# Attention with its shifted scores between the weighings, key blocks added in pairs on GpSimd, and a feed-forward stage written out without a loop

## The chip, the cores and the metric

The kernel runs on one core of a Trainium2 chip. The metric is the device time of one execution in microseconds (us). Of the kernel before, three runs gave 2557.92, 2559.57 and 2560.83 us, a median of 2559.57 us.

## The reference

One transformer layer with adaptive layer norms. `x` has 4 batches of 1024 rows of 512 numbers, there are 16 heads of 32, and the hidden width is 2048. Everything is fp32. Cut to what matters:

```python
h = layernorm(x) * (1 + ca) + sa
q = rotary((layernorm(h) @ Wq + bq) * scale, h); k, v = ...   # same for keys
qn, kn = layernorm(q), layernorm(k)                            # over each head's 32
scores = einsum('bhqd,bhkd->bhqk', qn, kn) / sqrt(32)
scores = where(causal, scores, -max)
a = softmax(scores) @ v
x = x + ga * (a @ Wo + bo)
h = layernorm(x) * (1 + cb) + sb
x = x + gb * ((silu(h @ w_gate.T) * (h @ w_up.T)) @ w_down.T)
```

## The kernel before

Each stage is a block of its own with one hand-written instruction stream per engine, tied by semaphores: setup and query/key/value projection, attention (`attention_stage`, about 443 to 1299 us of the span), output projection with the second layer norm, and the feed-forward stage (`ffn_stage`, from 1466 us to the end).

**Attention** works on 16 groups (one batch, four heads), one round per group. A round has 12 steps. In step `w` TensorE does, for the current group, two score items (`score`, L739, into the PSUM slots of `b_psA`); VectorE takes the maximum of each over its keys (`peak`, L820). For the group before, 14 steps later (`SHIFT_LAG`), it computes the scores again transposed and shifted by each row's maximum, one (half of the queries, block of 128 keys) per step, four heads (`shift`, L760 and L763, into the two buffers of `b_psB`); ScalarE takes the exponential of each head into `b_probT` (`exponent`, L887). One step later TensorE multiplies these weights with the values (`weigh(.., False)`, output `b_psO`) and with ones (`weigh(.., True)`, output `b_psL`, the sum of the weights, which is the softmax's divisor), both on L778. A block is 512, 384, 256 or 128 queries wide, by the causal mask: over the 12 blocks of a round six are 512 wide and two each have the other widths. The four heads lie in four column strips of the array, 32 columns each.

The order on TensorE in a step is: shift of heads 0 and 1, score, shift of heads 2 and 3, score, in steps 1 and 3 also eight transposes for the next group (`prepare`, L724), then the two products of `weigh`. After the last block of a half VectorE copies `b_psO` out (`take`, L836), in steps 7 and 3; it does so behind the first `peak` of its step. The transposes use a slot of `b_psA`, are widened on ScalarE (`widen`, L876), split into high and low part on GpSimd (`high`, L691) and VectorE (`low`, L813). The slots of `b_psA` are two and go round over scores, transposes and maxima, so each waits for the reader of the one before the last. When the sums of a group are out, GpSimd issues a chain of DMAs that turns them for a reciprocal and spreads the result (`normalise`, L695 to L705), and multiplies the output.

**Feed-forward** takes 8 row blocks of 512 rows; each goes over 16 hidden chunks of 128. A chunk is 24 matmuls for gate and up (`matrix`, L1286 to L1288) and, two chunks later, 12 for the down product (`down`, L1274 to L1276), which add up in `f_psD` over the 16 chunks. ScalarE does silu (L1217) and the high part of the product (L1212), VectorE the product (L1227) and its low part (L1231), GpSimd the split of the down weights. The loop over blocks is a hardware loop with peeled ends (`stagger`). At the border of two blocks the next block's rows are split all at once (`split_h`, L1207 and L1238) into the only buffer `f_hT_hi`/`f_hT_lo`, once the last chunk's up product is done; the last `down` of a block comes one chunk earlier than the others (`down_last`), and the end of a block (`final`, L1248 and L1250) scales and adds four tiles in turn, with two buffers for the scaled ones.

Of the kernel before, what the change touches and what calls it, by code (L numbers as in the profile page):

```python
# [26 lines left out]
P = 128  # L27
# [488 lines left out]
def attention_stage(nc, args, scratch):  # L516
# [12 lines left out]
    BUFS = 3  # L529

# [21 lines left out]

    def take_at(k):
# [15 lines left out]
    with ExitStack() as ctx:  # L569
# [3 lines left out]
        def sem(name):  # L573
# [18 lines left out]
        probT = sb("b_probT", [P, 3, 4, W])  # L592
# [9 lines left out]
                 "peaks_turned peaks_copied peaks_in shifted expd weighed summed taken_o taken_l sums_out few_in inverted few_out "  # L602
# [17 lines left out]
        def _(sp):  # L620
# [36 lines left out]

            load(0)
# [4 lines left out]
            for k in STEPS:  # L663
                n, w = unit(k)
                if peaks_at(k) is not None:
                    lay_peaks(peaks_at(k))
                if w == 4 and n + 2 < NG:
                    load(n + 2)
                if w == 4 and n + 1 < NG:
                    lay_stacks(n + 1)  # L670
                if w == 5 and 0 <= n < NG:
                    load_v(n)
                if w == 10 and 0 <= n - 2 < NG:
                    store(n - 2)
# [3 lines left out]
        def _(pool):  # L678
# [13 lines left out]

            def normalise(n):
                pool.wait_ge(s["taken_l"], 2 * n + 2)
                pool.dma_start(scratch["sums"][0], sums[0:P:HD, n % 2]).then_inc(s["sums_out"], 16)  # L695
                pool.wait_ge(s["sums_out"], 16 * n + 16)
                pool.dma_start(few[:, 0], scratch["sums"][0].rearrange("j (a c) -> (j a) c", c=C // HD)).then_inc(s["few_in"], 16)
                pool.wait_ge(s["inverted"], n + 1)
                pool.dma_start(scratch["sums"][1].rearrange("j (a c) -> (j a) c", c=C // HD), few[:, 1]).then_inc(s["few_out"], 16)
                pool.wait_ge(s["few_out"], 16 * n + 16)  # L700
                for j in range(4):
                    pool.dma_start(sums[j * HD:(j + 1) * HD, n % 2], scratch["sums"][1, j:j + 1].broadcast_to([HD, C])).then_inc(s["wide_in"], 16)
# [4 lines left out]
            for k in STEPS:  # L707
                if prep_at(k):
                    high(*prep_at(k))
                at = take_at(k)  # L710
                if at and at[1] == 1 and at[0] < NG - 1:
                    normalise(at[0])

        @block.tensor
        def _(pe):
# [50 lines left out]
            def weigh(n, w, summing):  # L766
                half, kb = BLOCKS[w]
                if not summing:
                    pe.wait_ge(s["expd"], 4 * (NW * n + w) + 4)
                    if w == 0:  # L770
                        pe.wait_ge(s["v_in"], 16 * n + 16)
                if kb == 0:
                    at_least(pe, s["taken_l" if summing else "taken_o"], 2 * n + half)
                first = max(kb, half * HALF)
                out = psL if summing else psO
                for j in range(4):
                    rows = slice(j * HD, (j + 1) * HD)
                    mm = pe.matmul(out[rows, (first - half * HALF) * P:W], ones[:] if summing else v[:, n % 2, kb, rows],  # L778
                                   probT[:, (NW * n + w) % 3, j, 0:(half + 1) * W - first * P],
                                   start=(kb == 0), stop=(kb == (half + 1) * HALF - 1), skip_group_check=True)  # L780
                mm.then_inc(s["summed" if summing else "weighed"], 1)

            for k in STEPS:
# [7 lines left out]
                if prep_at(k):  # L791
                    prepare(*prep_at(k))
                if peaks_at(k) is not None:
                    turn_peaks(peaks_at(k))
                if weigh_at(k):
                    weigh(*weigh_at(k), False)
                    weigh(*weigh_at(k), True)

        @block.vector
        def _(dve):  # L800
# [48 lines left out]
            for k in STEPS:  # L849
# [10 lines left out]
                at = take_at(k - 5)  # L860
                if at and at[1] == 1 and at[0] < NG - 1:
                    dve.wait_ge(s["few_in"], 16 * at[0] + 16)
                    dve.reciprocal(few[:, 1], few[:, 0]).then_inc(s["inverted"], 1)
                at = take_at(k)
# [4 lines left out]
        def _(act):  # L869
# [9 lines left out]
            def exponent(n, w, j):  # L879
# [3 lines left out]
                if j == 0:  # L883
                    at_least(act, s["summed"], NW * n + w - 2)
                    at_least(act, s["weighed"], NW * n + w - 2)
                width = (half + 1) * W - max(kb, half * HALF) * P
                act.activation(probT[:, (NW * n + w) % 3, j, 0:width], psB[:, i % 2, 0:width], ACT.Exp).then_inc(s["expd"], 1)  # L887
# [6 lines left out]
            def take(n, half):  # L894
                act.wait_ge(s["summed"], NW * n + (HALF if half == 0 else NW))
# [3 lines left out]
            for k in STEPS:  # L899
                for j in range(4):  # L900
                    if shift_at(k):
                        exponent(*shift_at(k), j)
                    if j == 1 and take_at(k):
                        take(*take_at(k))
# [207 lines left out]
def ffn_stage(nc, args, scratch, w_hi, w_lo, out):  # L1112

    NB = NT // 4
    T = 4 * P
    HC = HID // P
    with ExitStack() as ctx:
# [3 lines left out]
        def sem(name):  # L1123
# [3 lines left out]
        hT_hi = sb("f_hT_hi", [P, KC, T], F32R)  # L1127
        hT_lo = sb("f_hT_lo", [P, KC, T], F32R)
# [8 lines left out]
        scaled = sb("f_scaled", [P, 2, DM])  # L1137
        x1 = sb("f_x1", [P, 4, DM])
        spots = sb("f_spots", [1, 4])
        still = sb("f_still", [1, 1])  # L1140
# [4 lines left out]
        names = ("gate_in h_in h_hi h_lo gate_mm up_mm silu gu gu_hi gu_lo wd_hi wd_lo down "  # L1145
                 "scaled final still").split()
        s = {n: sem("f_" + n) for n in names}
        wd_in = [sem(f"f_wd_in{j}") for j in range(2)]
        x1_in = sem("f_x1_in")
# [3 lines left out]
        def done(i, c):  # L1153
            return i * HC + (c + 1)

        @block.sync
        def _(sp):
            def load_h(i, c):
                if c == 0:
                    at_least(sp, s["h_lo"], KC * i)  # L1160
# [201 lines left out]
```

## Time and profile before

| | |
|---|---|
| median of 3 runs | 2559.57 us |
| profiled execution | 2558.22 us |
| its span | 2556.4 us |
| mean granted TensorE clock | 0.964 |
| TensorE matmul busy | 2351.2 us (92%) |
| VectorE busy | 1178.3 us (46%) |
| ScalarE busy | 787.0 us (31%) |
| GpSimd busy | 752.0 us (29%) |

Busy time is the time in which an engine had at least one instruction under way. Matmuls overlap each other by their modelled ends, so on TensorE the distance from one start to the next says what an instruction costs, and its own duration does not. "Granted clock" is the share of TensorE's full clock in that stretch.

### The profile page before, as it was taken

The page shows a single profiled execution, that of the slowest core. Times are in us where ns is not written, and L with a number is a line of the kernel's source. Part 1 is how long each engine was busy: PE and PEld are TensorE (multiplying, and loading weights), DVE is VectorE, ACT ScalarE, POOL GpSimd, SP SyncE. Part 2 cuts the span into 40 slices and gives each one's busy share as a digit, 9 for nine tenths or more (in the row PEclk, how much of TensorE's full clock was granted, in tenths as well). Part 3 has the DMA queues.
Part 4 walks back from the last instruction along what each step waited for, and adds up shares of the span by engine and source line. Part 5 has one row for each costly group of instructions (what it writes and reads, how often), then busy time and mean ns, then how long its engine had stood idle before and what let it go on. Part 6 is the DMA issues. An engine that isn't in the chain of part 4 may idle for free. (4 is left out here: it accounts for less than half of the span.)

```text
span 2556.4 us, 33412 instructions
## 1 busy us (share of the span) xinstructions
PE 2351.2 (92%) x12504; PEld 1699.5 (66%) x12504; DVE 1178.3 (46%) x1806; ACT 787.0 (31%) x1659; POOL 752.0 (29%) x822
## 2 busy tenths in 40 slices
PE   2899995599999999999958799999999999999998
PEld 0677774466566566556436578787878787878787
DVE  4799996545555555555349721212121212121212
ACT  1333331054454545544535511111111111111111
POOL 1477776001211111121156322222222222222221
PEclk7899997589999999999989999999999999999999
DMA  5122222636545544643058721212121121212111
GB/s 181 59 99 99 98 90 104 140 76 146 122 102 126 134 110 108 140 118 89 19 172 295 259 83 31 87 33 78 38 66 49 45 70 45 70 46 69 41 59 36
DMA packets 162516, 244.80 MB, mean 96 GB/s; under 512 B 17205, under 2 KB 84373, under 8 KB 161902
## 3 DMA queue, kind: packets, MB, share of 16 engines
q1 hardware_dynamic: 153898, 222.23, 30.0%
q0 software_dynamic: 7456, 18.07, 2.6%
q10 hardware_dynamic: 1064, 3.18, 0.3%
q8 instruction: 64, 1.05, 0.2%
q14 instruction: 34, 0.28, 0.0%
HBM read 133.28 MB, written 59.28 MB: 75 GB/s over the span
## 5 line engine op out<-in xcount | busy, mean ns | idle before, releaser
L820 DVE TENSOR_REDUCE b_top<-b_psA 128x2 f32<-128x1024 f32 (+3 forms) x384 | 363.4, 957 | 289.6 <-PE b_psA L739 165.7
L887 ACT ACTIVATE b_probT<-b_psB 128x512 f32<-128x512 f32 (+3 forms) x768 | 339.7, 491 | 349.4 <-PE b_psB L763 234.0
L1227 DVE TENSOR_TENSOR f_gu<-f_psU,f_silu 128x512 f32<-128x512 f32 x128 | 88.5, 691 | 749.3 <-PE f_psU L1288 749.3
L760 PE MATMUL b_psB<-b_stack 98*128 98x512 f32 (+3 forms) x768 | 288.0, 414 | 6.3 <-ACT b_probT L887 4.9
L739 PE MATMUL b_psA<-b_stack 96*128 96x512 f32 (+3 forms) x768 | 256.6, 392 | 28.6 <-DMA b_stack<-b_halves 20.3
L760 PEld LDWEIGHTS b_psB<-b_stack 98*128 98x128 f32 x768 | 140.1, 189 | 190.1 <-issue 118.5
L57 POOL TENSOR_TENSOR f_spots<-f_still 1x1 f32<-1x1 f32 x128 | 25.9, 202 | 795.1 <-PE f_psD L1276 788.8
L1217 ACT ACTIVATE f_silu<-f_psG 128x512 f32<-128x512 f32 x128 | 76.6, 598 | 523.5 <-PE f_psG L1288 523.5
L1274 PE MATMUL f_psD<-f_wd_hi,f_gu_hi 128*128 128x512 f32 x512 | 201.1, 393 | 22.8 <-DVE f_gu_lo L1231 12.3
L1286 PE MATMUL f_psG<-f_hT_hi,w_hi 128*128 128x512 f32 x512 | 200.4, 391 | 11.1 <-DVE f_hT_lo L1238 11.1
L1276 PE MATMUL f_psD<-f_wd_hi,f_gu_lo 128*128 128x512 f32 x512 | 200.0, 391 | 0.0
L1287 PE MATMUL f_psG<-f_hT_hi,w_lo 128*128 128x512 f32 x512 | 199.9, 390 | 0.0
L1275 PE MATMUL f_psD<-f_wd_lo,f_gu_hi 128*128 128x512 f32 x512 | 199.8, 390 | 0.0
L1288 PE MATMUL f_psG<-f_hT_lo,w_hi 128*128 128x512 f32 x512 | 199.7, 390 | 0.0
L1287 PE MATMUL f_psU<-f_hT_hi,w_lo 128*128 128x512 f32 x512 | 199.2, 389 | 0.0
L1288 PE MATMUL f_psU<-f_hT_lo,w_hi 128*128 128x512 f32 x512 | 199.2, 389 | 0.0
L1286 PE MATMUL f_psU<-f_hT_hi,w_hi 128*128 128x512 f32 x512 | 199.2, 389 | 0.0
L1212 ACT ACTIVATE f_gu_hi<-f_gu 128x512 fp32r<-128x512 f32 x128 | 80.8, 631 | 358.3 <-DVE f_gu L1227 358.3
L739 PEld LDWEIGHTS b_psA<-b_stack 96*128 96x128 f32 x768 | 145.8, 201 | 45.7 <-issue 21.7
L1196 POOL TENSOR_TENSOR f_wd_lo<-f_wd,f_wd_hi 128x512 fp32r<-128x512 f32 x128 | 167.9, 1311 | 10.7
L778 PE MATMUL b_psO<-b_probT,b_v 128*32 128x512 f32 (+3 forms) x1536 | 164.3, 500 | 3.7 <-DVE b_att L836 2.8
L507 PE MATMUL a_psQ<-wqkv_hi,hT_hi 128*128 128x512 f32 x384 | 162.1, 422 | 0.0
(165 smaller groups left out, 4229.0 us busy)
## 6 DMA issues: line engine op xcount, KB each, us to landing
b_stack<-b_halves SPq DMA_DIRECT2D x192, 256.0 KB, 5.0
f_wd<-in_wd_t SPq DMA_DIRECT2D x128, 256.0 KB, 2.6
qkv_d<-a_t SPq DMA_DIRECT2D x32, 512.0 KB, 2.6
b_land<-qkv_d SPq DMA_DIRECT2D x32, 512.0 KB, 4.7
a_x<-in_x SPq DMA_DIRECT2D x32, 256.0 KB, 3.2
qkv_d<-a_v SPq DMA_DIRECT2D x32, 256.0 KB, 2.9
b_v<-qkv_d SPq DMA_DIRECT2D x16, 512.0 KB, 5.8
att_d<-b_att SPq DMA_DIRECT2D x16, 512.0 KB, 3.2
```

What stands on the lines that cost most here:

```text
L739: mm = pe.matmul(out[:, h, 0:hi - lo], stack[0:ROWS, n % BUFS, 1, j, t * P:(t + 1) * P], stack[0:ROWS, n % BUFS, 0, j, lo:hi], start=True, ...
L760: mm = pe.matmul(psB[:, i % 2, cols], stack[0:NR, n % BUFS, 0, j, kb * P:(kb + 1) * P], stack[0:NR, n % BUFS, 1, j, first * P:(half + 1) * ...
L778: mm = pe.matmul(out[rows, (first - half * HALF) * P:W], ones[:] if summing else v[:, n % 2, kb, rows], probT[:, (NW * n + w) % 3, j, 0:(h ...
L820: dve.tensor_reduce(out, slot("score", NI * n + i)[:, :, 0:width], AX.X, ALU.max, negate=True).then_inc(s["maxed"], 1)
L887: act.activation(probT[:, (NW * n + w) % 3, j, 0:width], psB[:, i % 2, 0:width], ACT.Exp).then_inc(s["expd"], 1)
L1196: pool.tensor_tensor(wd_lo[:, c % 2], wd[:, c % 2], wd_hi[:, c % 2].bitcast(F32), ALU.subtract).then_inc(s["wd_lo"], 1)
L1274: pe.matmul(out_t, gu_hi[:, c % 2, cols], wd_hi[:, c % 2], start=first, stop=False)
L1275: pe.matmul(out_t, gu_hi[:, c % 2, cols], wd_lo[:, c % 2], start=False, stop=False)
L1276: last = pe.matmul(out_t, gu_lo[:, c % 2, cols], wd_hi[:, c % 2], start=False, stop=end)
L1286: pe.matmul(out_c, w_hi[:, m, k, cols], hT_hi[:, k], start=(k == 0), stop=False)
L1287: pe.matmul(out_c, w_lo[:, m, k, cols], hT_hi[:, k], start=False, stop=False)
L1288: last = pe.matmul(out_c, w_hi[:, m, k, cols], hT_lo[:, k], start=False, stop=(k == KC - 1))
```

## The change

There are three edits in the attention stage and one rewrite of the feed-forward stage.

First, in a step `weigh` now stands behind the first score, between the two pairs of shifted scores; transposes and maxima stay behind the second score. Second, GpSimd adds the weights of the second key block of each pair into those of the first (`add_pair`, six adds a round, over 384, 128, 512, 512, 384 and 128 columns of each of four heads), and TensorE multiplies the sum with ones once for both (`add_up`), at the end of the even steps, three steps after the pair's second block. `b_probT` gets five buffers for three. Third, the DMAs of `normalise` move from GpSimd's queue to SyncE's (steps 6, 7, 9 and 10), its multiplication to step 11, the reciprocal to step 8, the store to step 2; the copy of the sums (`take` on ScalarE) comes two steps later.

In the feed-forward stage the loop is written out over all 128 chunks. `f_hT_hi` and `f_hT_lo` get two buffers, and the next block's split is spread over chunks 8 to 11. All `down` products come two chunks behind. The four scalings stand in chunk 1 of the next block, each behind its own tile's last matmul, the four additions in chunk 2, with four buffers. The rows to add land in `f_land`, which the split has left free by then.

```diff
+    PROBS = 5
+    def sum_at(k):
+        return pair_at(k - 3)
+    def take_sum_at(k):
+        return take_at(k - 2)
...
+            def add_pair(n, i):
...
+                pool.wait_ge(s["weighed"], NW * n + 2 * i + 1)
+                pool.wait_ge(s["expd"], 4 * (NW * n + 2 * i + 1) + 4)
+                pool.tensor_tensor(into, into, probT[:, (at + 1) % PROBS, :, 0:width], ALU.add).then_inc(s["added"], 1)
...
+            def add_up(n, i):
+                half, kb = BLOCKS[2 * i]
+                pe.wait_ge(s["added"], NW // 2 * n + i + 1)
+                if kb == 0:
+                    at_least(pe, s["taken_l"], 2 * n + half)
+                first = max(kb, half * HALF)
+                for j in range(4):
+                    mm = pe.matmul(psL[j * HD:(j + 1) * HD, (first - half * HALF) * P:W], ones[:],
...
-                if prep_at(k):
-                    prepare(*prep_at(k))
-                if peaks_at(k) is not None:
-                    turn_peaks(peaks_at(k))
-                if weigh_at(k):
-                    weigh(*weigh_at(k), False)
-                    weigh(*weigh_at(k), True)
+                    if i == 1 and prep_at(k):
+                        prepare(*prep_at(k))
+                    if i == 1 and peaks_at(k) is not None:
+                        turn_peaks(peaks_at(k))
+                    if i == 0 and weigh_at(k):
+                        weigh(*weigh_at(k))
+                if sum_at(k):
+                    add_up(*sum_at(k))
...
-        hT_hi = sb("f_hT_hi", [P, KC, T], F32R)
-        hT_lo = sb("f_hT_lo", [P, KC, T], F32R)
+        hT_hi = sb("f_hT_hi", [P, 2, KC, T], F32R)
+        hT_lo = sb("f_hT_lo", [P, 2, KC, T], F32R)
...
-            stagger(dve, NB, HC, [(product, 1), (split_h, 0), (low, 1), (final, 2)])
+            for u in range(NU + 3):
+                i, c = u // HC, u % HC
+                if 1 <= u <= NU:
+                    product(u - 1)
+                    low(u - 1)
+                if i < NB - 1 and 8 <= c < 8 + KC:
+                    split_h(i + 1, c - 8)
+                if c == 1 and 1 <= i <= NB:
+                    for t in range(4):
+                        scale(i - 1, t)
+                        if i == NB:
+                            add(i - 1, t)
+                if c == 2 and 1 <= i < NB:
+                    for t in range(4):
+                        add(i - 1, t)
...
-            stagger(pe, NB, HC, [(down_early, 2), (down_last, 1), (gate_up, 0)])
+            for u in range(NU + 2):
+                if u >= 2:
+                    down(u - 2)
+                if u < NU:
+                    at_least(pe, s["silu"], u - 1)
+                    matrix(u, 0)
+                    at_least(pe, s["gu"], u - 1)
+                    matrix(u, 1)
```

TensorE's queue in step 7 of a round, before (the names are the tiles of the text; L760 shift, L739 and L742 score, L778 the two products, first block of the second half):

```order
L760 MATMUL b_psB<-b_stack 128x512 [waits b_expd] x2
L739 MATMUL b_psA<-b_stack 128x384 [waits b_maxed]
L742 MATMUL b_psA<-b_mask_r,b_ident_r 128x128
L739 MATMUL b_psA<-b_stack 128x384
L742 MATMUL b_psA<-b_mask_r,b_ident_r 128x128
L760 MATMUL b_psB<-b_stack 128x512 [waits b_expd] x2
L739 MATMUL b_psA<-b_stack 128x512 [waits b_maxed]
L742 MATMUL b_psA<-b_mask_r,b_ident_r 128x128
L739 MATMUL b_psA<-b_stack 128x512
L742 MATMUL b_psA<-b_mask_r,b_ident_r 128x128
L778 MATMUL b_psO<-b_probT,b_v 32x512 [waits b_taken_o,b_expd]
L778 MATMUL b_psO<-b_probT,b_v 32x512 x3
```

The same step in the changed kernel (L800 shift, L779 and L782 score, L816 the product with the values):

```order
L800 MATMUL b_psB<-b_stack 128x512 [waits b_expd] x2
L779 MATMUL b_psA<-b_stack 128x384 [waits b_maxed]
L782 MATMUL b_psA<-b_mask_r,b_ident_r 128x128
L779 MATMUL b_psA<-b_stack 128x384
L782 MATMUL b_psA<-b_mask_r,b_ident_r 128x128
L816 MATMUL b_psO<-b_probT,b_v 32x512 [waits b_taken_o,b_expd]
L816 MATMUL b_psO<-b_probT,b_v 32x512 x3
L800 MATMUL b_psB<-b_stack 128x512 [waits b_expd] x2
L779 MATMUL b_psA<-b_stack 128x512 [waits b_maxed]
L782 MATMUL b_psA<-b_mask_r,b_ident_r 128x128
L779 MATMUL b_psA<-b_stack 128x512
L782 MATMUL b_psA<-b_mask_r,b_ident_r 128x128
```

The product with the values, and with it the wait for `b_taken_o` (VectorE's copy of `b_psO`), has moved from the end of the step to directly behind its first score. VectorE's queue at that place is the same in both kernels, here of the changed one (L871 the maxima, L887 the copy); the last of the seven maxima is that of the step's first score:

```order
L871 TENSOR_REDUCE b_top<-b_psA 128x2 [waits b_scored] x7
L887 COPY b_att<-b_psO 128x512 [waits b_stored,b_scaled,b_weighed]
L871 TENSOR_REDUCE b_top<-b_psA 128x2 [waits b_scored] x3
L914 RECIPROCAL b_few<-b_few 128x32 [waits b_few_in]
```

VectorE's queue at the border of two feed-forward blocks, before (L1248 scaling, L1250 addition, L1227 product, L1231 its low part):

```order
L1248 TENSOR_TENSOR f_scaled<-f_psD,f_gate 128x512 [waits f_down,f_x1_in,f_gate_in]
L1250 TENSOR_TENSOR f_x<-f_x,f_scaled 128x512 [waits f_scaled]
L1248 TENSOR_TENSOR f_scaled<-f_psD,f_gate 128x512
L1250 TENSOR_TENSOR f_x<-f_x,f_scaled 128x512 [waits f_scaled]
L1248 TENSOR_TENSOR f_scaled<-f_psD,f_gate 128x512 [waits f_final]
L1250 TENSOR_TENSOR f_x<-f_x,f_scaled 128x512 [waits f_scaled]
L1248 TENSOR_TENSOR f_scaled<-f_psD,f_gate 128x512 [waits f_final]
L1250 TENSOR_TENSOR f_x<-f_x,f_scaled 128x512 [waits f_scaled]
```

And in the changed kernel (L1310 scaling, L1315 addition, L1296 product, L1300 its low part):

```order
L1310 TENSOR_TENSOR f_scaled<-f_psD,f_gate 128x512 [waits f_down_t,f_gate_in]
L1310 TENSOR_TENSOR f_scaled<-f_psD,f_gate 128x512 [waits f_down_t] x2
L1310 TENSOR_TENSOR f_scaled<-f_psD,f_gate 128x512 [waits f_down]
L1296 TENSOR_TENSOR f_gu<-f_psU,f_silu 128x512 [waits f_gu_hi,f_silu,f_up_mm]
L1300 TENSOR_TENSOR f_gu_lo<-f_gu,f_gu_hi 128x512 [waits f_gu_hi]
L1315 TENSOR_TENSOR f_land<-f_land,f_scaled 128x512 [waits f_scaled,f_x1_in] x4
```

The four scalings no longer alternate with the additions, and the additions come a chunk later.

## Rows read from the trace of the kernel before

**Rows 1.** Each engine by stretch: start:end, length, busy, PE clock, DMA.

```profile
700.00:800.00 100.00, 98.87 (x750) 59.91 (x752) 54.82 (x66) 49.69 (x107) 17.10 (x21) 1.00 0.49 118
1600.00:1700.00 100.00, 96.73 (x426) 79.48 (x425) 24.62 (x36) 16.59 (x28) 25.14 (x36) 1.00 0.21 64
```

**Rows 2.** TensorE in time, a block border: start, us, engine, line, operation, count.

```profile
1602.91 0.39 PE L1276 MATMUL f_psD<-f_wd_hi,f_gu_lo 128*128 128x512 f32 x1
1605.07 0.50 PE L1274 MATMUL f_psD<-f_wd_hi,f_gu_hi 128*128 128x512 f32 x1 [1.77 <-DVE f_gu_lo L1231]
...
1618.58 0.39 PE L1288 MATMUL f_psU<-f_hT_lo,w_hi 128*128 128x512 f32 x1
1620.46 0.47 PE L1274 MATMUL f_psD<-f_wd_hi,f_gu_hi 128*128 128x512 f32 x1 [1.50 <-DVE f_scaled L1248]
```

**Rows 3.** ScalarE in time, two chunks of the feed-forward stage.

```profile
1626.22 0.60 ACT L1217 ACTIVATE f_silu<-f_psG 128x512 f32<-128x512 f32 x1 [3.91 <-PE f_psG L1288]
1634.38 0.60 ACT L1217 ACTIVATE f_silu<-f_psG 128x512 f32<-128x512 f32 x1 [4.08 <-PE f_psG L1288]
```

**Rows 4.** The chain that ended last: start, us, engine, tile, line.

```profile
2548.22 0.24 PE f_psD L1276
...
2553.29 0.69 DVE f_x L1250
```

**Rows 5.** GpSimd in time, once a round, two rounds.

```profile
764.46 1.04 POOL L691 TENSOR_SCALAR b_halves<-b_whole 128x1024 fp32r<-128x1024 f32 x1 [12.22 <-ACT b_whole L876]
...
813.87 1.04 POOL L691 TENSOR_SCALAR b_halves<-b_whole 128x1024 fp32r<-128x1024 f32 x1 [12.40 <-ACT b_whole L876]
```

**Rows 6.** TensorE in time, step 9 of a round.

```profile
793.14 0.99 PE L760 MATMUL b_psB<-b_stack 98*128 98x512 f32 x2
...
794.32 0.23 PE L742 MATMUL b_psA<-b_mask_r,b_ident_r 128*128 128x128 f32 x1
794.48 1.06 PE L778 MATMUL b_psO<-b_probT,b_v 128*32 128x512 f32 x8
795.36 1.04 PE L778 MATMUL b_psL<-b_probT,b_ones 128*32 128x512 f32 x8
796.33 0.50 PE L760 MATMUL b_psB<-b_stack 98*128 98x512 f32 x1
```

**Rows 7.** TensorE and VectorE in time, step 3 of a round.

```profile
767.95 0.73 PE L739 MATMUL b_psA<-b_stack 96*128 96x512 f32 x2
768.72 1.23 DVE L820 TENSOR_REDUCE b_top<-b_psA 128x2 f32<-128x1024 f32 x1 [0.49 <-PE b_psA L739]
769.86 0.68 DVE L836 COPY b_att<-b_psO 128x512 f32<-128x512 f32 x1
770.00 1.09 PE L724 MATMUL b_psA<-b_ident,b_land 128*128 128x128 f32 x8 [0.32 <-DVE b_top L820]
```

**Rows 8.** The same, step 7.

```profile
783.32 0.34 PE L739 MATMUL b_psA<-b_stack 96*128 96x384 f32 x1
784.92 0.68 DVE L836 COPY b_att<-b_psO 128x512 f32<-128x512 f32 x1
785.75 1.07 PE L778 MATMUL b_psO<-b_probT,b_v 128*32 128x512 f32 x8 [0.18 <-DVE b_att L836]
```

**Rows 9.** VectorE in time, step 4: low part, then the maxima.

```profile
774.70 2.08 DVE L820 TENSOR_REDUCE b_top<-b_psA 128x2 f32<-128x1024 f32 x2
```

**Rows 10.** Groups by line: busy us, mean ns, idle before.

```profile
L705 POOL TENSOR_TENSOR b_att<-b_att,b_sums 128x1024 f32<-128x1024 f32 x15 | 35.6, 2372 | 38.4 <-DMA b_sums<-sums_d 38.4
L352 POOL TENSOR_TENSOR a_t<-a_t,a_hmean 128x1024 f32<-128x1024 f32 x32 | 61.3, 1916 | 3.9
L1196 POOL TENSOR_TENSOR f_wd_lo<-f_wd,f_wd_hi 128x512 fp32r<-128x512 f32 x128 | 167.9, 1311 | 10.7
```

**Rows 11.** TensorE in time, the rounds' tail, without scores.

```profile
1272.70 0.73 PE L760 MATMUL b_psB<-b_stack 98*128 98x512 f32 x2
1273.88 0.50 PE L760 MATMUL b_psB<-b_stack 98*128 98x512 f32 x1 [0.45 <-ACT b_probT L887]
```

More of the change, by code:

```diff
@@ L902, in _ @@
                         exponent(*shift_at(k), j)
[L903 to L904 removed]
+                    if j == 1 and take_sum_at(k):
+                        take(*take_sum_at(k))
                 if prep_at(k):
@@ L1136, in ffn_stage @@
         gate = sb("f_gate", [P, DM])
[L1137 to L1140, printed above, removed]
+        scaled = sb("f_scaled", [P, 4, DM])
         psG = ctx.enter_context(nc.psum_tensor("f_psG", [P, 2, T], F32))
@@ new lines, in high, with gated @@
+            def high(u):
+                act.wait_ge(s["gu"], u + 1)
+                at_least(act, s["down"], u - 1)
+                act.activation(gu_hi[:, u % 2], gu[:, u % 2], ACT.Copy).then_inc(s["gu_hi"], 1)
+            def gated(u):
+                act.wait_ge(s["gate_mm"], u + 1)
+                at_least(act, s["gu"], u - 1)
+                act.activation(silu[:, u % 2], psG[:, u % 2], ACT.Silu).then_inc(s["silu"], 1)
+            for k in range(KC):
+                split_h(0, k)
@@ new lines, in low, with scale @@
+            def low(u):
+                dve.wait_ge(s["gu_hi"], u + 1)
+                dve.tensor_tensor(gu_lo[:, u % 2], gu[:, u % 2], gu_hi[:, u % 2].bitcast(F32), ALU.subtract).then_inc(s["gu_lo"], 1)
+            def scale(i, t):
+                if t == 0:
+                    dve.wait_ge(gate_in, 16 * (i // 2 + 1))
+                    at_least(dve, s["final"], 4 * i)
+                if t < 3:
+                    dve.wait_ge(s["down_t"], 3 * i + t + 1)
+                else:
+                    dve.wait_ge(s["down"], HC * (i + 1))
+                dve.tensor_tensor(scaled[:, t], psD[:, t], gate[:], ALU.mult).then_inc(s["scaled"], 1)
@@ new lines, in add @@
+            def add(i, t):
+                dve.wait_ge(x1_in, 16 * i + 16)
+                dve.wait_ge(s["scaled"], 4 * i + t + 1)
+                dve.tensor_tensor(x1[:, t], x1[:, t], scaled[:, t], ALU.add).then_inc(s["final"], 1)
+            for k in range(KC):
+                split_h(0, k)
+            for u in range(NU + 3):
+                i, c = u // HC, u % HC
+                if 1 <= u <= NU:
+                    product(u - 1)
+                    low(u - 1)
+                if i < NB - 1 and 8 <= c < 8 + KC:
+                    split_h(i + 1, c - 8)
+                if c == 1 and 1 <= i <= NB:
+                    for t in range(4):
+                        scale(i - 1, t)
[4 more added lines that the diff above has]
+                        add(i - 1, t)
```

270 lines of the change are left out of this document (139 added, 131 removed).

## The prediction

> **What bounds the kernel now.** I read the page first (TensorE busy 92%, no other engine half so much), then the busy time by stretch. In the attention stage TensorE is busy 98.87% of a 100 us stretch at granted clock 1.00, with VectorE and ScalarE near half and GpSimd at 17%; in the feed-forward stage it is 96.73% [rows 1]. So TensorE's queue sets the end in both, and an edit is worth what it takes from that queue or adds to it as a wait. Third, TensorE's instructions in time. The distance between starts is the cost there. In the feed-forward stage one chunk takes 1634.38 - 1626.22 = 8.16 us, 0.227 us for each of 36 matmuls [rows 3], which nothing interrupts but the borders of blocks. An attention round takes 813.87 - 764.46 = 49.41 us [rows 5].
>
> **Feed-forward: the borders.** At a border TensorE stands twice. The last down product waits for the low part of the last chunk, which stands on VectorE behind the next block's split: 1605.07 - 1602.91 - 0.23 = 1.93 us. Two chunks later the first down product waits for four tiles to be scaled and added in turn: 1620.46 - 1618.58 - 0.23 = 1.65 us [rows 2]. Together 3.6 us, at 7 borders 25 us. In the changed order the splits are spread over chunks 8 to 11, into another buffer, so the low part has nothing ahead of it, and a down product has a whole chunk of 8.16 us for it. The four scalings (0.7 us each) follow product and low part, some 5.3 us into a chunk, and are wanted at its end, at 8.16 us. Both waits go, and nothing I find is late next: the loads of down weights run two chunks ahead, and SyncE's waits for the stores are over within one. At the very end the last addition begins at 2553.29, 5.1 us behind the last matmul (2548.22) [rows 4]: four scalings and additions. Three of the four tiles can now begin 2.1 us before that matmul ends (nine matmuls of 0.23 us), which gives 2 us. Feed-forward: 25 + 2 = -27 us. Bounds: -14, if one of the two waits were to come back in another place, and -29, if the first matmuls behind each wait, a few hundredths slower, count too.
>
> **Attention: what goes, per round.** The product with ones for a 512-wide block costs 795.36 - 794.48 = 0.88 us, seen on the product of the same size before it [rows 6], so 0.22 us for each 128 queries. A round had 36 such units and keeps 20: 16 x 0.22 = -3.5 us. The old waits go too. The second pair of shifted scores waits for an exponential: the pair spans 0.99 us [rows 6] where a free pair spans 0.73 us [rows 11], and it begins about 0.1 us late; over the four full blocks in mid-round, and less in the others, I count 1.7 us. The transposes in step 3 wait about 0.4 us for the maxima (0.32 us is noted), and the product in step 7 about 0.25 us for the copy [rows 7, 8]. Sum of waits that go: -2.4 us.
>
> **What comes, per round.** First, switching. Between a matmul on the full array and one on a 32-column strip the row shows 0.16 us where a 128-wide matmul needs 0.07, and on the way back 796.33 - 795.36 = 0.97 us where the same product took 0.88 [rows 6]: 0.09 each way. The two products stood together and paid this once a step; six more islands a round cost 6 x 0.18 = +1.1 us. The Trainium skill (TensorEngine Tiling, Key Properties) says that changing the tiling mode drains the engine. The trace agrees, with 0.09 us for each change; whoever counts columns alone leaves these 1.1 us out.
>
> Second, the copy of `b_psO`. The product with the values of a half's first block waits for VectorE's copy of the half before, and that copy stands behind the maximum of the step's first score. So far the product came at the end of the step. Now it is directly behind the first score. In step 3 the score starts at 767.95, its maximum at 768.72, the copy at 769.86, lasting 0.68 us [rows 7], and the product can follow 0.15 us after the copy (785.60 to 785.75) [rows 8]: 2.74 us behind the score's start, of which the score takes 0.5 and the switch 0.1. That is a wait of 2.1 us. In step 7 the product would stay at 785.75, 2.43 us behind the score's start at 783.32 [rows 8], with 0.7 us of it worked: 1.75 us. Behind the product in TensorE's queue stand the second pair of shifted scores and the second score, so all of it is lost: +3.8 us. Third, transposes. After those of step 3 the maxima of step 4 begin at 774.70, 4.70 us after the transposes (770.00) [rows 7, 9], because VectorE waits for GpSimd's high part first; the first of them is over at 5.8 us, and only then may TensorE write the first score of step 5. It used to be later than that itself. Without the two products that stood behind the transposes it gets there after 1.0 + 3.6 + 0.5 = 5.1 us and waits 0.7. In step 2 the exponentials queue behind the widening of the transposes (+0.5), and at the ends of steps 4, 7 and 9, which have no product with ones, they are late by 0.1 to 0.3 each (+0.7). Sum +1.9 us.
>
> **GpSimd's adds** are 4 x (384 + 128 + 512 + 512 + 384 + 128) = 8192 columns a round. The nearest row, a sum-like two-input operation beside VectorE's maxima, takes 2372 ns for 1024 columns, 2.32 ns each; others show 1.87 and 2.56 [rows 10]. So 19 us, 15 to 21, with 2.1 us of high parts and 2.4 of multiplication, in a round of some 50. A full pair of 4.75 us has three steps, over 11 us, before its product. I count it at nothing.
>
> **Sum.** A round: -3.5 - 2.4 + 1.1 + 3.8 + 1.9 = +0.9 us; over 15 overlapped rounds +14 us. The tail of 14 steps without scores is different: no maximum stands before the copy, and the exponential waits of 0.45 us [rows 11] are covered by the product between the pairs. There: -3.5 + 1.1, six full steps x -0.45, 1 us more in narrow ones, +1 for the last add: -5 us. Attention +9, feed-forward -27: -18 us. Against the profiled execution's 2558.22 us that is 2540; the median of the runs shown is 1.35 us above it, so I predict 2542 us.
>
> **Rivals.**
> - *The copy is no wait (0.18).* The 3.8 us vanish, if VectorE's copy comes before the maximum, or if TensorE's later work hides them. For it: TensorE's record before shows only 0.18 us of this wait [rows 8]. Against it: both queues are fixed orders and the product now stands right behind the score. Then a round changes by -2.9 us: -44 - 5 - 27 = -76, 2483 us.
> - *The chain behind the transposes is longer (0.17), slower than before.* Place: VectorE's low part in steps 2 and 4, which holds up two maxima and with them both slots. I took a wait for step 4 alone. It decides when a round grows by more than (27 + 5) / 15 = 2.1 us, 1.2 more than in my sum. Were TensorE to wait for the full 4.7 us of [rows 7, 9] less the 3.3 us of shifted scores and products in between, at both places, that is 2 x 1.4 = 2.8 us more: 15 x 2.8 = 42, 2584 us.
> - *GpSimd sets the pace (0.05), slower.* From the end of step 7 to the next high part are about 24 us, with 5632 columns and 2.4 us of multiplication in them, so 3.9 ns a column decide, half as much again as the slowest row [rows 10]. At 4.6 ns a round gains 4 to 5 us: about 2610. The Trainium skill (GPSIMD Engine Reference, Specifications) has GpSimd share its SBUF interfaces with VectorE where that reads two SBUF inputs. VectorE's low part is the only such operation in a round, so this could touch few of the adds.
> - *Only half of the feed-forward's gain (0.10).* -14 there: 2555 us, no difference that can be told.
>
> The forecast itself has 0.50, between 2528 and 2556 us. I call 0.2% (5 us) the smallest change that can be told from none here. Faster: the forecast save its upper edge, and the first rival, 0.68; within 0.2%: 0.13; slower: 0.19. The range, 2500 to 2584 us, leaves out the full price of the first and third rival.
>
> **What would show it.** The row of the feed-forward stretch near 100% busy and both waits at the border gone, the chunk still 8.16 us. In attention a round of about 50.3 us in GpSimd's high parts; TensorE's product in steps 3 and 7 released by VectorE's copy, about 2 us each; six products with ones a round; TensorE released by maxima in step 5. I am wrong if a round is under 48 or over 52 us, if an add of 2048 columns takes over 8 us, or if a new wait stands in the feed-forward stage.

## The result: 12% slower, and the profile after

The changed kernel takes 2865.7 us (median of four runs, of which three took 2844.8 to 2866.4) against 2560.2 us before: ratio 1.116, 95% interval 1.110 to 1.1225. The fourth run, 3502.0 us at a granted clock of 0.63, is left out of the ratio. The forecast was 2542 us, in a range of 2500 to 2584. The profiled execution's span is 2862.8 us, its mean granted clock 0.874 (0.964 before).

In short: the feed-forward stage gained what was forecast. Attention lost 337 us in the traces. TensorE stands behind VectorE, partly for the copies that were forecast and partly because VectorE itself stands while certain GpSimd operations run, and TensorE's clock is low behind these stands.

First, where the time is. Each engine by stretch in the kernel after: start:end, length, busy time of TensorE, of its weight loads, VectorE, ScalarE and GpSimd, the granted clock, DMA share, GB/s.

```profile
900.00:1000.00 100.00, 85.83 (x474) 50.01 (x472) 49.00 (x46) 37.87 (x80) 35.01 (x12) 0.79 0.35 86
2000.00:2100.00 100.00, 100.00 (x443) 82.81 (x442) 25.34 (x36) 17.31 (x29) 23.73 (x24) 1.00 0.21 66
```

The feed-forward stage did what was forecast: 100% busy for 96.73% [rows 1]. From its first gate matmul to its last addition it takes 2860.4 - 1810.2 = 1050.2 us, before 2554.0 - 1473.2 = 1080.8: 30.6 us less. All of the loss is in attention, where TensorE was busy 98.87% at clock 1.00 [rows 1] and is now busy 86% at 0.79. GpSimd in time, its high part of the queries once a round (start, us):

```profile
942.03 1.04 POOL L728 TENSOR_SCALAR b_halves<-b_whole 128x1024 fp32r<-128x1024 f32 x1 [11.61 <-ACT b_whole L927]
...
1013.88 1.04 POOL L728 TENSOR_SCALAR b_halves<-b_whole 128x1024 fp32r<-128x1024 f32 x1 [11.11 <-ACT b_whole L927]
```

A round takes 71.85 us where it took 49.41 [rows 5]: 22.4 us more, and 15 of them are the 337 us by which the feed-forward stage starts later.

Second, which waits. What TensorE waited for in the whole kernel: us in total, times, longest.

```profile
PE b_psA L779 <- DVE b_top L871: 69.8, 35, 4.7
PE b_psO L816 <- DVE b_att L887: 54.1, 29, 2.0
PE b_psA L789 <- DVE b_top L871: 51.4, 14, 3.8
```

In time, one round of TensorE: the copy waits of steps 7 and 3, the turned peaks in step 0, the first score of step 5.

```profile
905.21 1.93 PE L816 MATMUL b_psO<-b_probT,b_v 128*32 128x512 f32 x8 [1.74 <-DVE b_att L887]
...
931.17 0.45 PE L789 MATMUL b_psA<-b_ident,b_peaks 128*128 128x128 f32 x1 [3.82 <-DVE b_top L871]
...
949.34 1.80 PE L816 MATMUL b_psO<-b_probT,b_v 128*32 128x512 f32 x8 [2.00 <-DVE b_att L887]
...
962.18 1.22 PE L779 MATMUL b_psA<-b_stack 96*128 96x512 f32 x2 [4.03 <-DVE b_top L871]
```

Two of the four were forecast, with their sizes (1.75 and 2.1). The two large ones were not: 3.8 us in step 0 at a place that the prediction never looked at, and 4.0 us in step 5 where it had 0.7.

Third, what is late there: VectorE, grouped by line and form in 600 to 1200 us of the kernel after (count, busy us, mean ns).

```profile
L864 DVE TENSOR_TENSOR b_halves<-b_whole,b_halves 128x1024 fp32r<-128x1024 f32 x17 | 58.5, 3441 | 50.3 <-POOL b_halves L728 50.3
L876 DVE TENSOR_TENSOR b_least<-b_top 128x32 f32<-128x32 f32 x8 | 18.3, 2283 | 0.3
L879 DVE CAST b_peaks<-b_least 128x32 fp32r<-128x32 f32 x8 | 18.0, 2251 | 0.3
```

In the kernel before, the same three lines in the same stretch:

```profile
L813 DVE TENSOR_TENSOR b_halves<-b_whole,b_halves 128x1024 fp32r<-128x1024 f32 x24 | 29.4, 1225 | 56.2 <-POOL b_halves L691 56.2
L825 DVE TENSOR_TENSOR b_least<-b_top 128x32 f32<-128x32 f32 x12 | 2.3, 192 | 0.4
L828 DVE CAST b_peaks<-b_least 128x32 fp32r<-128x32 f32 x12 | 2.2, 182 | 0.4
```

Nothing in these instructions changed, and an operation of 32 columns takes twelve times as long. What runs beside them, in the timeline of after (GpSimd's addition L738 and multiplication L743, VectorE's `b_least`, cast and low part):

```profile
924.66 3.46 POOL L738 TENSOR_TENSOR b_probT<-b_probT 128x1536 f32<-128x1536 f32 x1 [3.54 <-ACT b_probT L942]
925.89 2.29 DVE L876 TENSOR_TENSOR b_least<-b_top 128x32 f32<-128x32 f32 x1
928.09 2.33 POOL L743 TENSOR_TENSOR b_att<-b_att,b_sums 128x1024 f32<-128x1024 f32 x1
928.21 2.25 DVE L879 CAST b_peaks<-b_least 128x32 fp32r<-128x32 f32 x1
930.49 0.19 DVE L881 TENSOR_TENSOR b_peaks<-b_least,b_peaks 128x32 fp32r<-128x32 f32 x1
...
956.47 3.44 POOL L738 TENSOR_TENSOR b_probT<-b_probT 128x1536 f32<-128x1536 f32 x1
956.54 4.45 DVE L864 TENSOR_TENSOR b_halves<-b_whole,b_halves 128x1024 fp32r<-128x1024 f32 x1 [2.63 <-POOL b_halves L728]
```

`b_least` ends at 928.18, the addition beside it at 928.12. The cast ends at 930.46, the multiplication at 930.42. The low part ends at 960.99, which is 1.08 us after the addition that began 0.07 us ahead of it (959.91). Each VectorE operation ends only after GpSimd's: by 0.06 and 0.04 us for the two small ones, which alone take 0.19 and 0.18, and by 1.08 for the low part, which alone takes 1.23. Maxima and copies that read PSUM keep their own times (1220 and 680 ns), and so do GpSimd's additions (4557, 3451 and 1279 ns for 2048, 1536 and 512 columns: 2.2 to 2.5 ns each, as forecast).

Fourth, the clock. Stretches of after around the two stands at 927 and 958 us:

```profile
927.00:931.00 4.00, 0.35 (x4) 0.20 (x2) 3.93 (x5) 0.35 (x2) 3.42 (x2) 0.76 0.00 0
931.00:942.50 11.50, 11.33 (x47) 7.61 (x47) 2.80 (x4) 3.14 (x8) 0.47 (x1) 0.50 0.17 48
...
953.00:958.00 5.00, 5.00 (x44) 3.47 (x43) 2.15 (x2) 2.44 (x6) 2.54 (x2) 1.00 0.54 159
...
962.10:970.00 7.90, 7.82 (x35) 5.28 (x36) 3.77 (x5) 1.84 (x5) 1.27 (x1) 0.50 0.97 198
```

TensorE stands 3.8 us and then works 11.5 us at 1.2 GHz instead of 2.4 (0.50 granted), although it is 98% busy there. It recovers, and falls again behind the next stand. So a wait costs its own length and, as an estimate from 0.50 granted, half of the stretch at the low clock behind it.

The round then adds up. Stands: 1.7 + 3.8 + 2.0 + 4.0 = 11.6 us (from the busy time, 600 to 1200 us, 500.26 of 600 in 8.35 rounds: 11.9 us). Work at full clock: 45.6 us, taken from a later run with the same order and no large stand (late_copy_first_chain: 582.71 of 600 us busy, round 46.93). The rest, 71.85 - 11.9 - 45.6 = 14.3 us, is the low clock.

### The profile page after: what moved, and what is told of

Its sections match the earlier page's. It is cut to its first block and busy times, and to the rows that moved or that the text cites. A ratio compares the mean times of both kernels' runs of the same rounds, so it can differ in the third digit from the quotient of the medians.

```text
span 2862.8 us, 31120 instructions
## 1 busy us (share of the span) xinstructions
PE 2515.6 (88%) x11736; PEld 1795.7 (63%) x11736; DVE 1307.0 (46%) x1806; ACT 792.6 (28%) x1659; POOL 975.6 (34%) x684
## 5 line engine op out<-in xcount | busy, mean ns | idle before, releaser
L871 DVE TENSOR_REDUCE b_top<-b_psA 128x2 f32<-128x1024 f32 (+3 forms) x384 | 362.9, 956 | 487.6 <-PE b_psA L782 406.3
L738 POOL TENSOR_TENSOR b_probT<-b_probT 128x1536 f32<-128x1536 f32 (+1 forms) x96 | 297.2, 3095 | 444.7 <-ACT b_probT L942 444.7
L1296 DVE TENSOR_TENSOR f_gu<-f_psU,f_silu 128x512 f32<-128x512 f32 x128 | 88.5, 692 | 711.9 <-PE f_psU L1363 711.9
L779 PE MATMUL b_psA<-b_stack 96*128 96x512 f32 (+3 forms) x768 | 323.0, 479 | 91.0 <-DVE b_top L871 69.8
L1252 POOL TENSOR_SCALAR f_wd_hi<-f_wd 128x512 fp32r<-128x512 f32 x128 | 83.5, 652 | 819.0 <-PE f_psD L1348 775.5
L800 PE MATMUL b_psB<-b_stack 98*128 98x512 f32 (+3 forms) x768 | 340.3, 497 | 4.7 <-ACT b_probT L942 3.9
L800 PEld LDWEIGHTS b_psB<-b_stack 98*128 98x128 f32 x768 | 173.8, 243 | 271.5 <-issue 151.1
L779 PEld LDWEIGHTS b_psA<-b_stack 96*128 96x128 f32 x768 | 186.8, 256 | 121.2 <-DVE b_top L871 77.4
L816 PE MATMUL b_psO<-b_probT,b_v 128*32 128x512 f32 (+3 forms) x1536 | 209.2, 624 | 54.5 <-DVE b_att L887 54.1
```

The lines of the kernel that those rows point to most:

```text
L738: pool.tensor_tensor(into, into, probT[:, (at + 1) % PROBS, :, 0:width], ALU.add).then_inc(s["added"], 1)
L779: mm = pe.matmul(out[:, h, 0:hi - lo], stack[0:ROWS, n % BUFS, 1, j, t * P:(t + 1) * P], stack[0:ROWS, n % BUFS, 0, j, lo:hi], start=True, ...
L800: mm = pe.matmul(psB[:, i % 2, cols], stack[0:NR, n % BUFS, 0, j, kb * P:(kb + 1) * P], stack[0:NR, n % BUFS, 1, j, first * P:(half + 1) * ...
L816: mm = pe.matmul(psO[rows, (first - half * HALF) * P:W], v[:, n % 2, kb, rows], probT[:, (NW * n + w) % PROBS, j, 0:(half + 1) * W - first ...
L871: dve.tensor_reduce(out, slot("score", NI * n + i)[:, :, 0:width], AX.X, ALU.max, negate=True).then_inc(s["maxed"], 1)
```

## Experiments

All intervals are 95%, against the kernel before timed beside them (2561.8 to 2563.3 us).

**ffn_only.** The kernel before with the changed feed-forward function alone.

> The attention stage of before with the feed-forward stage of the change. Prediction's step: both waits at 7 borders and part of the end go, -27 to -30 us, so 2530 us. Rival (the new stage is part of the loss): not under 2555 us. The two traces so far, from the first gate matmul to the last addition, have 1081 and 1050 us.

Measured 2532.0 us, ratio 0.988 [0.986, 0.990]. The half that was forecast to gain gains 31 us by itself; attention must lose 334.

**tiny_adds.** The changed kernel, each addition on one column per head. It leaves the rest of every second key block out of the divisors.

```diff
-pool.tensor_tensor(into, into, probT[:, (at + 1) % PROBS, :, 0:width], ALU.add)
+pool.tensor_tensor(into[:, :, 0:1], into[:, :, 0:1], probT[:, (at + 1) % PROBS, :, 0:1], ALU.add)
```

> The changed kernel, but GpSimd adds one column per head in each pair instead of all (the divisors of the softmax leave the rest out). Order, semaphores and TensorE's work stay. Theory 1 (GpSimd's long adds hold up VectorE's low parts and the small operations on the maxima; TensorE then stands for 4 us, its clock falls): low parts back to 1.23 us, the operations on the maxima at 0.19 us, granted clock over 0.95, a round near 50.3 us, total 2520 to 2550 us. Theory 2 (the waits for VectorE's copy, 2 us twice a round, are what lowers the clock): the copy waits stay and the clock stays near 0.75 in attention, total over 2750 us.

Measured 2664.1 us, ratio 1.040 [1.037, 1.042]. Some 200 us go with the additions' length alone, while every instruction and every semaphore stays: low part 1226 ns, cast 182 ns. The time lies between the two theories and 114 us above the first one's range. Part of what is left is seen: `b_least` still takes 1302 ns on average, held by the normalising multiplication, which ends beside it (0.04 us before it in the round at 793 us); the copy waits are still 54.2 us; and VectorE stands 54.0 us in 14 waits for `b_few`, of which more below.

**late_adds.** The changed kernel with GpSimd's additions in full, but held until VectorE's low part (steps 1 and 3) or the peaks (last step) are done.

```diff
                 pool.wait_ge(s["expd"], 4 * (NW * n + 2 * i + 1) + 4)
+                if behind is not None:
+                    pool.wait_ge(s[behind[0]], behind[1])
...
+                    if prep_at(k):
+                        behind = ("lo_done", 2 * prep_at(k)[0] + prep_at(k)[1] + 1)
+                    if score_at(k) and score_at(k)[1] == NW - 1:
+                        behind = ("peaks_ready", 3 * score_at(k)[0] + 3)
```

> The changed kernel, but GpSimd begins the adds of steps 1 and 3 behind VectorE's low part and the add of step 11 behind the work on the maxima. All adds are done. Theory 1: no VectorE operation is held up, clock over 0.95, 2520 to 2560 us. Theory 2 (copy waits) or theory 3 (the load of 19 us of adds as such, by GpSimd's pace or memory traffic): no better than 2750 us.

Measured 2626.8 us, ratio 1.027 [1.023, 1.030]: 239 us below the change with the same additions (4.55, 3.46 and 1.28 us), now not beside those operations (1226, 192 and 182 ns). The multiplication stands behind the last addition in GpSimd's queue and moved with it, so the 239 us are the price of both. It is the place of the additions that costs, and not the load: all of them are done here, and the time is 37 us below tiny_adds. The range of theory 1 (up to 2560 us) is missed by 67 us all the same. The copy waits stand as before (54.2 us in 29), VectorE stands 48.3 us in 14 waits for `b_few`, and the clock is at 0.92 between 600 and 1200 us.

**add_beside_low.** The reverse: the kernel before, and behind the high part in steps 1 and 3 an addition of 2048 columns on a buffer that nothing else uses.

```diff
                     high(*prep_at(k))
+                    if prep_at(k)[0] >= 1:
+                        at_least(pool, s["extra"], 2 * prep_at(k)[0] + prep_at(k)[1] - 2)
+                        pool.tensor_tensor(extra[:, 1], extra[:, 0], extra[:, 0], ALU.add).then_inc(s["extra"], 1)
```

> The kernel before, with one independent GpSimd addition of 2048 columns of a tile of its own in steps 1 and 3, directly behind the high part, so that it runs when VectorE wants to make the low part. Nobody waits for it. Theory 1: each low part lasts 4.5 us or more instead of 1.23 (it waits for the add's end), rounds 1 to 5 us longer, 2575 us or more, lower clock if TensorE's stands grow to about 4 us. Theory 3: low part stays at 1.23 us and the time at 2560 us.

Measured 2682.7 us, ratio 1.047 [1.045, 1.048]. VectorE and GpSimd in time (the low part is L819, the extra addition L715):

```profile
813.41 3.59 POOL L715 TENSOR_TENSOR b_extra<-b_extra 128x2048 f32<-128x2048 f32 x1
...
813.47 4.62 DVE L819 TENSOR_TENSOR b_halves<-b_whole,b_halves 128x1024 fp32r<-128x1024 f32 x1 [2.27 <-POOL b_halves L694]
```

No data joins the two. The low part ends 1.09 us behind the addition (817.00), TensorE waits up to 3.31 us for the maxima behind it in the middle rounds (5.8 us once, at the start), and `b_least`, with no addition beside it, keeps its 193 ns. This shows the cause by itself: 120 us in the kernel before, or 8 us a round where 1 to 5 were expected, from two low parts of 4.6 us. In the change the additions beside them are shorter (512 and 1536 columns), so the 120 us are not its share there.

**scale_beside_low.** The same with one input: `pool.tensor_scalar(extra[:, 1], extra[:, 0], 1.0, 1.0, ALU.mult, ALU.mult)`.

> The kernel before with one more GpSimd operation behind the high part in steps 1 and 3, on a buffer of its own, as in the run with an addition there (2682.7 us; low part 1.23 -> 4.6 us), but with one input in place of two: a scaling of 2048 columns. If any long GpSimd operation holds VectorE's operations of two inputs: low part 3 to 4.6 us, time above 2640 us. If it is only GpSimd's operations of two inputs: low part 1.23 us as before, time 2560 to 2575 us.

Measured 2612.1 us, ratio 1.019 [1.018, 1.021].

```profile
794.71 1.91 POOL L715 TENSOR_SCALAR b_extra<-b_extra 128x2048 f32<-128x2048 f32 x1
...
794.77 2.91 DVE L819 TENSOR_TENSOR b_halves<-b_whole,b_halves 128x1024 fp32r<-128x1024 f32 x1 [3.04 <-POOL b_halves L694]
```

Below the time that the first theory gave (over 2640), and the low part a little below its 3 to 4.6 us, but by its mechanism: the low part ends 1.06 us behind the scaling (796.62). The expectation had taken the scaling to be as long as the addition; it takes 1.9 us, and so it holds for less. A one-input GpSimd operation holds VectorE as a two-input one does, and for as long as it lasts itself.

**copy_first.** The changed kernel, and VectorE copies `b_psO` ahead of the maximum of the step's first score.

```diff
+if i == 0 and take_at(k):
+    take(*take_at(k))
 if score_at(k):
     n, w = score_at(k)
     peak(n, 2 * w + i)
-if i == 0 and take_at(k):
-    take(*take_at(k))
```

> The changed kernel with only VectorE's copy moved ahead of the maximum. The holding up of VectorE by GpSimd's adds stays. If both causes add up, this gains what late_adds_copy_first gains on late_adds (some 120 us): 2740 us. If the long stands of 4 us alone keep the clock low, it gains only the 3.8 us a round, at most 60 us: 2800 us or more.

Measured 2756.3 us, ratio 1.077 [1.075, 1.078]: 109 us less than the change, 7.3 us a round, for waits of 3.74 us. It lies between the two theories, nearer to the first, but the 120 us that this one took over from late_adds_copy_first came out there as 34 (2626.8 to 2592.5, below).

**order_only.** The kernel before, with both products (values and ones) behind the first score in place of the step's end.

> The kernel before, with both products of weigh behind the step's first score instead of at the step's end; no pairs, old feed-forward stage. By the sum of the prediction the copy waits cost 3.8 us a round and the waits that go give 2.4 us: about +1.4 us a round, 2580 us at full clock. If stands of 2 us twice a round lower the clock by themselves: over 2610 us, with granted clock under 0.95 in attention.

Measured 2692.5 us, ratio 1.050 [1.048, 1.053]. No addition, no pair: 130 us lost by the place alone. The waits in it:

```profile
PE b_psO L778 <- DVE b_att L836: 54.2, 29, 2.0
```

**order_only_copy_first.** The same with the copy ahead of the maximum.

> The kernel before with both products behind the first score (2692.5 us with the old place of the copy), and VectorE's copy of psO put ahead of the maximum. If the copy waits of 1.7 and 2.0 us and the clock that falls behind them made all of those 130 us: 2550 to 2590 us, clock 0.96. If the order itself costs (switching of the array's form, transposes crowded behind one another): over 2630 us.

Measured 2591.4 us, ratio 1.011 [1.010, 1.013], just over the upper end of the first theory. Clock 0.99 in 600 to 1200 us (0.91 without it). So 101 of the 130 us were the copy waits of 54 us in all: nearly two for one. The other 29 us are 1.9 us a round (pitch 51.27), in which TensorE's records note 0.81, 0.89, 0.26 and 0.29 us of waits for maxima and the copy. Of the 2.4 us of waits that were to go, the 1.7 us for the exponentials did not go with this order. The wait moved from the second pair of shifted scores to the first pair of the next step, which now spans 0.96 us, while the second spans 0.72:

```profile
744.59 0.72 PE L760 MATMUL b_psB<-b_stack 98*128 98x512 f32 x2
...
745.80 0.96 PE L760 MATMUL b_psB<-b_stack 98*128 98x512 f32 x2
```

**late_adds_copy_first.** Both cures in the changed kernel.

> late_adds, and VectorE copies the product's sum before the maximum of the same step instead of behind it. If the copy waits of 2 us, twice a round, are what still lowers the clock and lengthens the round, the clock comes to over 0.98 in attention and a round to 46 to 47 us: 2480 to 2510 us. Rival: the waits behind the transposes, which stay, hold the clock down: above 2570 us.

Measured 2592.5 us, ratio 1.012 [1.010, 1.014]. A miss: the two causes do not make up the whole.

**pairs_old_order_late**, with the product also back at the end of the step:

> late_adds, but the product with the values stands at the end of the step as before. No copy waits (VectorE has the whole step), no more switches of the array than before. By the sum: -3.5 us a round for the products with ones, up to +1.9 us for the waits behind the transposes, feed-forward -29 us: 2480 to 2510 us, clock over 0.98 in attention. Rival: waits behind the transposes lower the clock, 2560 us or more.

Measured 2548.9 us, ratio 0.995 [0.993, 0.997], a miss too, 17 us above ffn_only. Both have a stand of TensorE of 3.0 to 4.6 us in nearly every round, and VectorE executes nothing in most of it. In time, in late_adds_copy_first (SyncE's transfers of the divisors, GpSimd's addition, VectorE, TensorE):

```profile
758.50 1.34 SPq L671 DMA_DIRECT2D sums_d<-b_sums  x1
...
761.62 4.50 POOL L740 TENSOR_TENSOR b_probT<-b_probT 128x2048 f32<-128x2048 f32 x1 [2.72 <-ACT b_probT L949]
...
763.51 0.35 SPq L675 DMA_DIRECT2D b_few<-sums_d  x1
765.19 0.35 DVE L921 RECIPROCAL b_few<-b_few 128x32 f32<-128x32 f32 x1 [7.49 <-DMA b_few<-sums_d]
765.46 1.75 DVE L878 TENSOR_REDUCE b_top<-b_psA 128x2 f32<-128x1024 f32 x2
...
766.68 1.22 PE L786 MATMUL b_psA<-b_stack 96*128 96x512 f32 x2 [4.58 <-DVE b_top L878]
```

A third cause. The change moved these transfers to SyncE's steps 6 and 7; the second waits for the landing of the first (5 us from start to start), and VectorE reaches its reciprocal in step 8 before the sums are in. Both maxima are queued behind it. In the changed kernel itself this wait is noted once, with 1.1 us: the slow rounds hid it. It comes up as the rounds get faster: 29.6 us in copy_first, 48.3 in late_adds, 54.0 in tiny_adds, 92.4 in late_adds_copy_first and 94.2 in pairs_old_order_late. The reciprocal itself, with one input, runs wholly inside GpSimd's addition (761.62 to 766.12) and keeps its 0.35 us, so not every VectorE operation beside GpSimd stands.

**old_order_late_chain** and **late_copy_first_chain.** These two versions with the divisors' path later (SyncE's transfers, GpSimd's multiplication, VectorE's reciprocal):

```diff
-                    if w == 9:
+                    if w == 10:
                         few_out(n - 2)
-                    if w == 10:
+                    if w == 11:
                         wide_in(n - 2)
...
-                if w == 11 and 0 <= n - 2 < NG - 1:
-                    normalise(n - 2)
+                if w == 0 and 0 <= n - 3 < NG - 1:
+                    normalise(n - 3)
...
-                if w == 8 and 0 <= n - 2 < NG - 1:
+                if w == 10 and 0 <= n - 2 < NG - 1:
                     dve.wait_ge(s["few_in"], 16 * (n - 2) + 16)
```

> The version with the additions held back and both products where they stood (2548.9 us), with one more edit: the reciprocal moves from step 8 to step 10, its transfers to steps 10 and 11, the normalising multiplication to step 0 of the next round. In its predecessor VectorE stood 94.2 us over 13 rounds, up to 8.2 us, at the reciprocal until the 32 sums had come in, and TensorE stood behind it for 4.4 us at a time. If that stand is the third cause: VectorE's wait for b_few falls under 10 us, attention runs at a clock of 0.98 or more, and the time is 2480 to 2500 us, which is the kernel with the new feed-forward stage alone (2532.0) less 15 rounds of 16 products of 0.22 us (52.8 us), plus up to 1 us a round of waits. If the stand is only a symptom and the pairs cost TensorE something else: 2530 to 2550 us, with the clock still about 0.95.

> The same edit on the version with the additions held back, VectorE's copy ahead of the maximum, and the product behind the first score as in the change (2592.5 us). If the reciprocal's wait is the last large cause there too: 2485 to 2515 us, above its neighbour with the old order only by the waits of 0.3 us in step 3 and 0.8 us in step 5 and the switching, at most 1.5 us a round. If the early place of the product has a cost of its own that has nothing to do with waits: over 2540 us.

Measured 2481.3 us, ratio 0.9675 [0.966, 0.969], and 2496.4 us, ratio 0.974 [0.973, 0.975]. Both lie in the expected ranges; the wait for `b_few` is gone from both lists. The multiplication moved as well, but its old place held up nothing that the traces show: the low part and the operations on the maxima had their own length in both predecessors (1226, 193 and 182 ns). Stretch of old_order_late_chain:

```profile
700.00:800.00 100.00, 99.14 (x703) 61.49 (x702) 58.56 (x69) 53.93 (x115) 49.32 (x21) 1.00 0.50 123
```

Its round is 748.66 - 702.59 = 46.07 us in GpSimd's high parts, 3.34 below [rows 5]; 15 x 3.34 = 50 us, which is what lies between it and ffn_only (2532.0 - 2481.3 = 51). This version beats both kernels, by 3.3% and by 13%, with the change's own ideas: pairs, additions on GpSimd, unrolled feed-forward. The product with the values is back at the end of its step. GpSimd does all its additions here with the clock at 1.00, so they do not lower the clock by themselves.

## Why the prediction was wrong, point by point

- **"Feed-forward: -27 us": right in its mechanism, a little small.** -30.6 in the traces, -31 alone, just outside its bound of -29. The end gave what was forecast, nearly: the last addition begins at 2859.71, 3.5 us behind the last matmul (2856.24), where it was 5.1 [rows 4]. The borders gave the other 29 us, 4.1 each in place of 3.6; what the 0.5 us are was not looked for.
- **"The product with ones ... 16 x 0.22 = -3.5 us": right.** 3.34 a round in old_order_late_chain, the version in which the product with the values keeps its old place.
- **"The copy of `b_psO` ... 3.8 us": the wait right (1.74 + 2.00), its price wrong.** Each stand was counted at its own length. This is the second term that failed. The runs give 101 us for 54 us of waits (order_only and its copy-first twin), 109 in the changed kernel: the clock falls behind a stand, and the work behind it takes up to twice as long.
- **"It gets there ... and waits 0.7": right, where nothing holds VectorE.** 0.80 us with both cures and the later chain. In the changed kernel it is 4.03.
- **"GpSimd's adds ... I count it at nothing": the step that failed.** The durations were right (4.56 us for 4.75), and GpSimd's own time has room, as was said. What was missing is what the additions do to VectorE. They run behind the high part in steps 1 and 3, which is just when VectorE's low part starts, and in step 11 beside `b_least` and the cast. Holding them back, with the multiplication, gives 239 us where the change lost 305 in all. A round of over 52 us was named as the sign of being wrong; it took 71.85.
- **The rival "GpSimd sets the pace"** touched the cause and turned it round. It asked whether the additions become slower, and found that few can. It named "VectorE's low part" as "the only such operation", and missed `b_least` and the subtraction, and the cast, which has only one input and stood as well. The additions keep their rate, VectorE stands. The Trainium skill (SBUF — State Buffer, SBUF: two separate sides) has this: an exclusive lock on the shared port pair, held for the whole instruction by whichever starts first, while the other blocks. The rows above agree with it in the one direction that they show, GpSimd first and VectorE blocked: 2.29 us for `b_least`, 2.25 for the cast. The prediction weighed only what the sharing does to GpSimd.
- **The rival "the chain behind the transposes is longer"** had the right place and the wrong size: steps 2 and 4, at 1.4 us each, at full clock, so 2584 us. The low part of step 4 made TensorE wait 4.03 us, since the part itself took 4.45.
- **Not forecast at all:** the divisors' path on SyncE. In the changed kernel it costs nearly nothing, in a version cured of the other two 96 us (2592.5 to 2496.4).
- **Priced so, the change comes out:** clean with its early product, a round of 46.93 us with the copy first, while the sum gave 49.41 + 0.9 - 3.8 = 46.5. The working was sound for the sum of the work in TensorE's queue and blind to what other engines do to one another, and to what a stand does to the clock. That its single terms (the 2.4 us of waits that go, the 1.1 of switching, the 1.2 at the exponentials) are right is not shown: no run takes one of them alone, and in order_only_copy_first the 1.7 us at the exponentials only moved.

The effects do not add up: from the change, the copy alone gives 109 us, the additions alone 239, both together 273, and the chain 96 more. Part of the 75 us missing from 348 is seen in the wait for `b_few`, which grows to 92.4 us when both are cured; with it gone the gain is 369 us.

What stays open: whether VectorE in turn holds GpSimd by a noticeable time here (no run was made for it; GpSimd's full additions keep their rate in every trace), and how the clock's loss divides among single stands, since only whole rounds were compared.

## What to carry to other kernels

An operation given to an idle engine is free only if nothing that the busy path needs runs beside it on a shared resource: before moving work to GpSimd, list VectorE's operations that read two SBUF tensors, or cast from SBUF to SBUF, at those moments, and put the long GpSimd operation behind them. Price a stand of TensorE at more than its length where the engine is otherwise full: the stands of 2 us cost about twice theirs here (101 us for 54). Cure all stands before judging an idea, since one that is left can hide its gain (2592.5 us with one left, 2496.4 without it). When a version becomes faster, look again at transfers with fixed steps: rounds that were slow hid them.

## What the runs showed of the hardware that was not expected

- A VectorE operation of 0.19 us stood 2.1 us beside a GpSimd operation, and the 1.23 us low part became 4.62; each ended 0.04 to 1.1 us behind the end of GpSimd's, and in add_beside_low no data joined the two. A reciprocal of 0.35 us with one input did not stand inside an addition of 4.50 us.
- GpSimd's one-input scaling of 2048 columns takes 1.91 us (0.93 ns a column). Its addition of a contiguous buffer to itself takes 3.59, and the kernel's additions of the same 2048 columns in four pieces 4.56.
- TensorE, 98% busy over 11.5 us, was granted 0.50 throughout behind a stand of 3.8 us. In late_adds_copy_first the 8 us from 764 on, which begin in a stand of 4.6 us, were granted 0.57; in its twin with the later chain, with no stand over 0.81 us in the middle rounds, 1.00 over 600 us.
